# A decoder's mixer stage: its output product from high and low parts instead of one fp32 product

## What is computed

```python
xn = _layernorm(x, ln_gamma, ln_beta)
k = einsum('btc,dc->btd', xn, Wk);  v = ... Wv;  r = ... Wr
td, tf = sigmoid(time_decay), sigmoid(time_first)
kv = k * v
csum = cumsum(kv * power(td, t), axis=1)          # along the tokens
shifted = csum moved by one token, 0 in front
wkv = tf * kv + td * shifted
out = einsum('btc,dc->btd', sigmoid(r) * wkv, Wo)
x = _layernorm(x + out)
```

## Time and profile before

| | us |
|---|---|
| three runs, median (lowest to highest) | 2070.69 (2066.13 to 2072.72) |
| the profiled execution | 2067.53 |
| its span, first to last instruction | 2065.8 |
| PE busy in the span | 1970.1 |
| DVE, ACT, POOL busy in the span | 1536.3, 1254.3, 1486.5 |

### The profile page before, as it was taken

How to read it: one execution, slowest core, us unless ns; L and a number is a source line. 1 busy time by engine, 2 the same in 40 slices (tenths; PEclk the granted TensorE clock), 3 DMA queues, 4 the chain that set the end, 5 groups by cost and what they waited for, 6 DMA issues and landing times. The chain is left out here.

```text
span 2065.8 us, 50743 instructions
## 1 busy us (share of the span) xinstructions
PE 1970.1 (95%) x14320; PEld 1770.5 (86%) x14320; DVE 1536.3 (74%) x3647; ACT 1254.3 (61%) x3478; POOL 1486.5 (72%) x1695
## 2 busy tenths in 40 slices
PE   8999799999999999788999999999999999699997
PEld 6888578888887888677999999999999999678886
DVE  7888567877877787765777788888888888535554
ACT  4565466566665666534777777777777777424443
POOL 5655423776776777665888888888888888669765
PEclk9999999999999999999999999999999999889999
DMA  4300114224224323305777767677766776467543
GB/s 141 98 0 0 36 62 160 87 83 154 91 82 135 110 82 130 105 22 176 235 237 236 244 230 243 219 234 241 240 228 225 244 227 231 163 254 245 194 164 102
DMA packets 244915, 330.03 MB, mean 160 GB/s; under 512 B 50074, under 2 KB 167234, under 8 KB 244836
## 3 DMA queue, kind: packets, MB, share of 16 engines
q1 hardware_dynamic: 218788, 279.97, 41.9%
q0 software_dynamic: 26048, 49.10, 6.5%
HBM read 236.17 MB, written 77.18 MB: 152 GB/s over the span
## 5 line engine op out<-in xcount | busy, mean ns | idle before, releaser
L1362 POOL DMA_INDIRECT slot_token<-a_entry,a_slot_i x256 | 260.9, 1019 | 114.4 <-issue 70.7
L1827 POOL DMA_INDIRECT part_rows<-e_out,e_dest x184 | 222.6, 1210 | 56.8 <-issue 52.2
L2387 POOL DMA_INDIRECT x<-x_rows,tok x188 | 205.9, 1095 | 70.8 <-issue 56.6
L1958 ACT ACTIVATE e_sg<-e_g 128x256 f32<-128x256 f32 x368 | 141.3, 384 | 180.8 <-PE e_g L1675 180.1
L2007 DVE TENSOR_TENSOR e_h<-e_sg,e_u 128x256 f32<-128x256 f32 x368 | 157.1, 427 | 103.6 <-ACT e_sg L1958 48.0
L1187 ACT ACTIVATE a_prob<-a_s,a_ntop 128x128 f32<-128x128 f32 x512 | 180.4, 397 | 3.0 <-DVE a_ntop L1547 2.8
L1835 POOL TENSOR_TENSOR e_wd1l<-x,e_wd1h 128x256 fp32r<-128x256 f32 x184 | 145.9, 831 | 6.6 <-ACT e_wd1h L1938 5.7
L1835 POOL TENSOR_TENSOR e_wd0l<-x,e_wd0h 128x256 fp32r<-128x256 f32 x184 | 146.2, 831 | 2.9 <-ACT e_wd0h L1938 2.0
L1049 PE MATMUL a_o<-a_wo,a_ot 128*128 128x256 f32 x512 | 123.1, 384 | 8.4 <-DVE a_ot L1614 8.4
L2022 DVE TENSOR_SCALAR e_out<-e_d,e_dest 128x256 f32<-128x256 f32 x184 | 80.6, 479 | 59.4 <-PE e_d L1675 58.9
L1187 ACT ACTIVATION_READ_ACCUMULATOR a_prob<-a_s,a_ntop 128x1 f32 x512 | 122.0, 238 | 0.0
(11 more groups left out here) (395 smaller groups left out, 7579.7 us busy)
## 6 DMA issues: line engine op xcount, KB each, us to landing
x<-in_eg SPq DMA_DIRECT2D x94, 512.0 KB
x<-in_eu SPq DMA_DIRECT2D x94, 512.0 KB, 5.6
x<-in_ed SPq DMA_DIRECT2D x93, 512.0 KB, 5.2
part_rows<-a_zero SPq DMA_DIRECT2D x16, 2048.0 KB
x<-part_rows SPq DMA_DIRECT2D x16, 2048.0 KB, 9.5
x<-in_x SPq DMA_DIRECT2D x16, 512.0 KB, 3.8
x_rows<-x SPq DMA_DIRECT2D x16, 512.0 KB, 3.8
out_rows<-x SPq DMA_DIRECT2D x16, 512.0 KB, 9.9
```

The source lines that it names most:

```text
L1362: pool.indirect_dma_start(k.slot_tok, bass.IndirectOffsetOnAxis(ap=slot_i[:, j, q:q + 1], axis=0), entry[:, j, q, :], None, bounds_check=S ...
L1827: pool.indirect_dma_start(k.part_d, bass.IndirectOffsetOnAxis(ap=dest[a][:, n, 1:2], axis=0), out[a][:, n, :], None).then_inc(put[a], 16)
L1958: act.activation(sg[m % 2][:], bank_g[m % 2][:, 0:SETW], ACT.Silu).then_inc(sg_rdy, 1)
L2387: pool.indirect_dma_start(k.xg[a][:, n, :], None, k.x2_d, bass.IndirectOffsetOnAxis(ap=k.tok[a][:, n, 0:1], axis=0)).then_inc(k.rows_in[a] ...
```

## The change

`mix` becomes a `split_product` for groups 0 to 14: y's high part is copied by ACT (`mixed_high`, 128x512, one for each half), the low part is subtracted by POOL (`mixed_low`, 128x512, y and its high part both in SBUF), and the weight's parts are made once (`outputs_high` on ACT, `outputs_low` on DVE). The last group keeps the plain fp32 product. y, doubled before, is one buffer now, so `gated(g, c)` waits for `mixed_low(g-1, c)` instead of for `mix`; the high and low parts are one buffer each, so `mixed_high` waits for the `mix` before. The raw weights of k, v and r give their space to the new tiles. The semaphore of the two first sigmoids is merged with that of the weights' high parts (the waits at L551 and L606 count accordingly).

```diff
-        w = {n: p.sb("w" + n, [P, DC, D]) for n in "kvro"}
+        w = {"o": p.sb("wo", [P, DC, D])}
+        with ExitStack() as opening:
+            for n in "kvr":
+                w[n] = opening.enter_context(nc.sbuf_tensor("m_w" + n, [P, DC, D], F32))
+        wo = [p.sb("wo" + h, [P, DC, D], F32R) for h in "hl"]
+        y_low = p.sb("yl", [P, DC, GW], F32R)
...
-        run, y = p.sb("run", [P, DC, GW]), [p.sb(f"y{i}", [P, DC, GW]) for i in range(2)]
-        cen, sq = y[1][0:G + E, 0, 0:D], y[1][0:G + E, 1, 0:D]
+        run, y = p.sb("run", [P, DC, GW]), p.sb("y", [P, DC, GW])
+        y_part = [p.sb("yh", [P, DC, GW], F32R), y_low]
+        cen, sq = y[0:G + E, 0, 0:D], y[0:G + E, 1, 0:D]
...
-                def mix(g, par, h):
+                def mix(g, h):
+                    whole = isinstance(g, int) and g == NG - 1
+                    if isinstance(g, int) and g == 0 and h == 0:
+                        pe.wait_ge(low_rdy, ONE + LOWS + 1)
                     if h == 0:
-                        pe.wait_ge(y_rdy, ONE + DC * (g + 1))
+                        pe.wait_ge(y_rdy if whole else yl_rdy, ONE + DC * (g + 1))
...
                     for j in range(2 * h, 2 * h + 2):
+                        out, toks = bank_o[h][:, (j % 2) * D:(j % 2 + 1) * D], slice(j * T, (j + 1) * T)
+                        if not whole:
+                            last = split_product(pe, out, [((y_part[0][:, q, toks], y_part[1][:, q, toks]),
+                                                            (wo[0][:, q, :], wo[1][:, q, :])) for q in range(DC)])
+                            continue
                         for q in range(DC):
-                            last = pe.matmul(bank_o[h][:, (j % 2) * D:(j % 2 + 1) * D], y[par][:, q, j * T:(j + 1) * T],
-                                             w["o"][:, q, :], start=(q == 0), stop=(q == DC - 1))
+                            last = pe.matmul(out, y[:, q, toks], w["o"][:, q, :], start=(q == 0), stop=(q == DC - 1))
...
+                def outputs_high():
+                    act.wait_ge(off_done, 2)
+                    act.wait_ge(w_in, DMA + 64)
+                    act.activation(wo[0][:], w["o"][:], ACT.Copy).then_inc(high_rdy, 1)
+
+                def mixed_high(g, c):
+                    act.wait_ge(y_rdy, ONE + DC * g + c + 1)
+                    if at_least(g, 1):
+                        act.wait_ge(o_done, ONE + 2 * g)
+                    act.activation(y_part[0][:, c, :], y[:, c, :], ACT.Copy).then_inc(yh_rdy, 1)
+
                 def period(g, par):
                     keys(g, 0)
...
+                    if at_least(g, 1):
+                        mixed_high(g - 1, 0)
                     gate(g, 0)
                     if more(g):
                         turned(g + 1, 1 - par)
...
+                    if at_least(g, 1):
+                        mixed_high(g - 1, 1)
                     keys(g, 1)
                     if more(g, 2):
                         norm_in(g + 2)
                     gate(g, 1)
+                    if isinstance(g, int) and g == 0:
+                        outputs_high()
...
-                def gated(g, par, c):
+                def gated(g, c):
                     pool.wait_ge(wkv_rdy, ONE + DC * g + c + 1)
                     pool.wait_ge(sr_rdy, ONE + DC * g + c + 1)
-                    if at_least(g, 2):
-                        pool.wait_ge(o_done, ONE + 2 * (g - 1))
-                    pool.tensor_tensor(y[par][:, c, :], run[:, c, :], sr[:, c, :], ALU.mult).then_inc(y_rdy, 1)
+                    if at_least(g, 1):
+                        pool.wait_ge(yl_rdy, ONE + DC * (g - 1) + c + 1)
+                    elif c == 0:
+                        pool.wait_ge(cen_t, 1)
+                    pool.tensor_tensor(y[:, c, :], run[:, c, :], sr[:, c, :], ALU.mult).then_inc(y_rdy, 1)
+
+                def mixed_low(g, c):
+                    pool.wait_ge(yh_rdy, ONE + DC * g + c + 1)
+                    pool.tensor_tensor(y_part[1][:, c, :], y[:, c, :], y_part[0][:, c, :].bitcast(F32), ALU.subtract)\
+                        .then_inc(yl_rdy, 1)
 
                 def period(g, par):
                     decayed(g, 0)
                     if not more(g):
                         context_low()
+                    if at_least(g, 1):
+                        mixed_low(g - 1, 0)
+                        mixed_low(g - 1, 1)
                     decayed(g, 1)
...
+                def outputs_low():
+                    dve.wait_ge(high_rdy, ONE + SIGMOIDS + 3 * DC + 1)
+                    dve.tensor_tensor(wo[1][:], w["o"][:], wo[0][:].bitcast(F32), ALU.subtract).then_inc(low_rdy, 1)
...
                     summed(g, 1)
+                    if isinstance(g, int) and g == 0:
+                        outputs_low()
```

More of the change, by code:

```diff
@@ L126, in mixer_stage @@
         vec_in, cen_in = p.sem("vec_in"), p.sem("cen_in")
-        fill, sig = p.sem("fill"), p.sem("sig")
+        fill = p.sem("fill")
         table, cent, cen_t = p.sem("table"), p.sem("cent"), p.sem("cen_t")
         FILLS, TABLES = 10, 4 + 3 * DC
-        w = {n: p.sb("w" + n, [P, DC, D]) for n in "kvro"}
+        w = {"o": p.sb("wo", [P, DC, D])}
[4 more added lines that the diff above has]
+        y_low = p.sb("yl", [P, DC, GW], F32R)
         parts = {n: [p.sb(f"w{n}{h}", [P, DC, D], F32R) for h in "hl"] for n in "kvr"}
@@ L154, in mixer_stage @@
         high_rdy, low_rdy, off_done, xl_rdy = (p.sem(n) for n in ("high", "low", "off_done", "xl"))
-        LOWS = 3 * DC + 3
+        SIGMOIDS, LOWS = 2, 3 * DC + 3
         mv_rdy, rs_rdy = p.sem("mv"), p.sem("rs")
@@ L161, in mixer_stage @@
         x1_rdy, kc_rdy = p.sem("x1"), p.sem("kc")
+        yh_rdy, yl_rdy = p.sem("yh"), p.sem("yl")
         OUT = 5
@@ L292, in period @@
                     if at_least(g, 1):
-                        mix(g - 1, 1 - par, 0)
-                        mix(g - 1, 1 - par, 1)
+                        mix(g - 1, 0)
+                        mix(g - 1, 1)
                 def offsets(names):
@@ L313, in _ @@
                 project_ahead(range(4))
-                mix(NG - 1, 1, 0)
-                mix(NG - 1, 1, 1)
+                mix(NG - 1, 0)
+                mix(NG - 1, 1)
                 project_ahead(range(4, 8))
@@ L319, in _ @@
             def _(act):
-                begin(act, xn_rdy, xnt_rdy, sr_rdy, kc_rdy, x1_rdy, high_rdy)
+                begin(act, xn_rdy, xnt_rdy, sr_rdy, kc_rdy, x1_rdy, high_rdy, yh_rdy)
                 def high_ahead(n):
@@ L399, in _ @@
                 act.wait_ge(vec_in, 64)
-                act.activation(k.td[:], td[:], ACT.Sigmoid).then_inc(sig, 1)
-                act.activation(k.tf[:], tf[:], ACT.Sigmoid).then_inc(sig, 1)
+                act.activation(k.td[:], td[:], ACT.Sigmoid).then_inc(high_rdy, 1)
+                act.activation(k.tf[:], tf[:], ACT.Sigmoid).then_inc(high_rdy, 1)
                 weights_high()
@@ L415, in _ @@
             def _(pool):
-                begin(pool, rs_rdy, w_rdy, y_rdy)
+                begin(pool, rs_rdy, w_rdy, y_rdy, yl_rdy)
                 def root(n, first, last):
@@ L463, in period @@
                         root(g + 3, 0 if more(g, 3) else TG, 2 * TG if at_least(g, 2) else TG)
-                    gated(g, par, 0)
-                    gated(g, par, 1)
+                    gated(g, 0)
+                    gated(g, 1)
                 pool.memset(k.ident[:], 0.0).then_inc(fill, 1)
@@ L550, in weights_low @@
                         for c in range(DC):
-                            dve.wait_ge(high_rdy, ONE + DC * i + c + 1)
+                            dve.wait_ge(high_rdy, ONE + SIGMOIDS + DC * i + c + 1)
                             dve.scalar_tensor_tensor(parts[n][1][:, c, :], w[n][:, c, :], k.gam[:, c:c + 1],
@@ L602, in period @@
                     summed(g, 1)
+                    if isinstance(g, int) and g == 0:
+                        outputs_low()
                 def decays():
-                    dve.wait_ge(sig, 2)
+                    dve.wait_ge(high_rdy, ONE + SIGMOIDS)
                     dve.wait_ge(fill, FILLS)
```

## The result

The changed kernel takes 2109.85 us (median of four runs, 2104.99 to 2113.21) against 2069.23 for the kernel before beside it: a ratio of 1.0186 (1.0170 to 1.0201). The forecast was 2090 with a range from 2078 to 2099. The sign was right; the forecast slowdown was about half of the measured one.

What follows compares the result with a forecast made beforehand. PE paces the mixer at 12.73 us a period; with the collision the POOL-DVE loop, 14.02, becomes the bound. 18.76 + 1.98 + 0.4 = 21.1 gives 2088.7 on the profiled execution, 2091.8 on the median; forecast 2090, range 2078 to 2099.

Steps and rivals of the forecast that it cites:

- The lock and its order: Mixer: POOL's subtractions and DVE's scan and product with tf exclude each other, POOL first, held engine next; loop 14.02 us.
- the scan and the product with tf are both held and not one of them: Against the rival that only one of the two subtractions collides: loop 12.7 to 12.8, time 2069 to 2073, chance 0.06.
- DVE doesn't go first: Against the rival that DVE goes first after decayed: loop 13.35, time 2079 to 2082, chance 0.16.
- its own work isn't the bound: Against the rival that PE's new matmuls come no closer than the old: period 14.5, time near 2090, chance 0.03.
- The mixer's sum: Mixer: fourteen loops from period 0's to period 14's scan of half 1, +18.76 us, then the last period, +1.98.
- PE's 24 matmuls: Output product on PE: 2.72 us instead of 3.46 for 16, so PE's period falls by 0.74 to 11.99 us.
- The loop without the collision: Mixer's loop between POOL and DVE, root to the next scan of half 1: 11.97 us with 8 columns.
- ACT's two copies: Two 128x512 copies of y a period on ACT, 0.71 us each: nothing, at most 0.7 us a period without cover.
- the first rival: Mixer: the subtractions don't collide and fit POOL's hole of 2.81 us; PE's 11.99 paces; 2058 to 2061, chance 0.09.
- The clock in the mixer: Mixer: PE's wait of some 2 us before each output product was put at nothing for PE's clock.
- the weight's low part on DVE ... +0.4: Period 0 of the mixer: outputs_low, 0.68 us, meets the root once; +0.4 us, between nothing and 0.7.
- the other edits ... cost nothing: One semaphore less, the tiles' places and one buffer for y were put at no cost.

Runs made afterwards that it cites:

- The run with bare subtractions: Kernel before plus two GpSimd subtractions per period between the two decayed, results unused, no other part of the change: 1.0055, 2081.55 us.
- the run without the subtractions: Changed kernel with one VectorE instruction less ahead of the mixer's loop and mixed_low cut to its signal, low part zero: 0.9973, 2065.56 us.
- 1, 2 and 32 bad, 48 and 64 good, 130 bad: VectorE instructions ahead of the attention loop beyond before (32: changed kernel plus 31); ratios in this order 1.0095, 1.0045, 1.0116 (mixer's cost included), 0.9996, 0.9988, 1.0033.

## Why the prediction was right, and where it was wrong

- **The lock and its order: right.** POOL goes first, and whoever was held goes next. Scan 2.30 (forecast some 2.3), product with tf 1.57 (some 1.7), PE idle 1.42 in the period shown and at most 1.7 (some 2), period 13.91 (14.02). The four rivals are out: the two engines don't read side by side, the scan and the product with tf are both held and not one of them, DVE doesn't go first, and PE idles, so its own work isn't the bound. The run with bare subtractions shows that the lock alone slows the loop: 11.0 of the 19.2 us, with shorter subtractions.
- **The mixer's sum: right.** 18.0 at period 14's scan (forecast 18.76), 19.2 at the last scan (20.7).
- **PE's 24 matmuls: 2.94 us instead of 2.72** behind a wait, with 0.23 for the first, and 2.87 without one (122.78 to 125.65 in the run without the subtractions). PE's own period is therefore 12.14, not 11.99. It didn't matter here, since the loop was later.
- **The loop without the collision: 12.33 instead of 11.97.** It runs through ScalarE, since root waits for ACT's x. That root waits there was in the rows (L430 "[2.05 <-ACT x L370]") and was read as idle time only. ACT's two copies, put at nothing, cost nothing in the changed kernel, where root doesn't wait for ACT, but they stand in this loop. It is why the best case was 0.4 us a period and not 0.74. Without the collision some 2064 comes out (0.9973 of 2069), not the first rival's 2058 to 2061.
- **The clock in the mixer: right.** PE's waits, 17.8 us in twelve with the longest at 1.7, left it at 1.00.
- **The step that failed: "the weight's low part on DVE ... +0.4" and "the other edits ... cost nothing".** outputs_low was costed by its duration and by what it meets. It was also one more instruction ahead of a loop, and that alone is worth 18 us. The sum ended where the mixer ends and took for granted that code that isn't changed keeps its time. The range was built from the mixer's unknowns alone, and what was left above it (0.08) was for a slower clock or a third collision in the mixer, so no case of it reached 2110. What the runs showed in its place: the stall at the attention loop's head, 14.7 us in five passes, and with it some 23 us of the stage.
- **What could have been read.** The list of DMA queues of before has instruction queues, with 41 packets on q14, and the loop of the attention stage has none of their packets between 450 and 840 us: its code stayed put. That one instruction more would end this could not be read from before; that instruction packets existed and the loop lived without them could, and was worth a rival with a price of its own.

## What to carry to other kernels

Count what a change does to the program as well as to the work: an instruction added ahead of a loop (shown here for VectorE) can make the loop's code come in anew on each pass, so look at the instruction queues of both profiles and at "issue" waits at the loop's head, and move the loop by a few dozen cheap instructions to tell this from everything else. Before work goes into a hole of GpSimd, look at what VectorE runs there: beside VectorE's instructions with two SBUF inputs it adds nearly its full time to theirs (a scan of 1.23 took 2.30 beside a subtraction of some 1.3), so such a hole isn't free.

## What the runs showed of the hardware

- The code of a loop can be loaded again on every pass. When the body of 303 VectorE instructions lies at a bad place, five packets of 8 KB come per pass, and the engine stands still for 1.7 us at the jump back, 2.9 at one place; at a good place none come. By the Trainium skill (Runtime: NRT & Kernel Launch, Instruction fetch mechanics) a taken branch to code outside the window that the engine holds must wait for a fetch; the runs agree with that (14.6 us in five jumps). The Trainium skill gives blocks of 16 KiB there; the packets here are of 8 KB, and the places (1, 2 and 32 bad, 48 and 64 good, 130 bad) go with blocks of that size.
- A stall grows on its way. 14.7 us on DVE became 12.7 us of waiting on PE, and that brought four stretches of 3.8 us at a clock of 0.55 to 0.63; the attention stage lost 23 us. Where the clock stayed at 1.00 behind the stalls, 8.3 to 8.9 us of stall cost some 6 to 9 us of time.
- A GpSimd copy with one SBUF input holds VectorE's scan (1.60 for 1.23) and is held by it (1.33 for 0.62).
